# One hand-written order for all engines of a transformer block, written anew for each kind of iteration

## The reference

```
x = attention(ln(x), ln(x), Wq1, Wkv1, Wo1) + x      # 16 heads of 16 columns, 1024 keys
x = attention(ln(x), ctx, Wq2, Wkv2, Wo2) + x        # 16 heads, 154 keys
h, g = split(ln(x) @ Wff1 + bff1)                    # 256 -> 2 x 1024
x = (h * g * sigmoid(1.702 * g)) @ Wff2 + bff2 + x
x = softmax((x @ Wq.T + bq) @ (ctx @ Wk.T + bk).T) @ (ctx @ Wv.T + bv) + x
```

## Time and profile before

| | |
|---|---|
| median of 3 runs | 1716.65 us (1714.28 to 1716.99) |
| span of the profiled execution, first to last instruction | 1710.7 us |
| iterations 9 to 15 (everything in them) | 96.7 to 96.9 us each |
| iterations 17 to 19 | 93.7 us each |
| iterations 5, 6, 7 | 75.9, 65.9, 72.3 us |
| tail | 160.7 us |
| ScalarE's copy of a values tile (lines 1101 and 1161), mean | 0.37 us |

### The profile page before, as it was taken

How to read it: one execution, slowest core, us unless ns; L and a number is a source line. 1 busy time by engine, 2 the same in 40 slices (tenths; PEclk the granted TensorE clock), 3 DMA queues, 4 the chain that set the end, 5 groups by cost and what they waited for, 6 DMA issues and landing times.

```text
span 1710.7 us, 33819 instructions
## 1 busy us (share of the span) xinstructions
PE 1609.0 (94%) x12897; PEld 1019.8 (60%) x12897; DVE 1120.2 (65%) x2221; ACT 996.5 (58%) x2024; POOL 269.4 (16%) x344
## 2 busy tenths in 40 slices
PE   6799999999999999999999999999999999998887
PEld 5444445575756666575756666565656556564666
DVE  4466786867667685867667685867677676824333
ACT  3345767656666666656666666556666566663332
POOL 5201312112102021111102021101010010101100
PEclk9989999999999999999999999999999999997789
DMA  6913241446231231346221231336030321303200
GB/s 175 231 46 121 72 79 58 105 85 136 58 79 46 65 77 51 91 96 136 58 70 41 72 77 42 91 74 135 27 84 23 62 60 38 78 20 76 54 26 13
DMA packets 171647, 129.37 MB, mean 76 GB/s; under 512 B 40751, under 2 KB 161885, under 8 KB 171229
## 3 DMA queue, kind: packets, MB, share of 16 engines
q1 hardware_dynamic: 171421, 127.19, 31.1%
q10 hardware_dynamic: 64, 0.02, 0.0%
HBM read 78.92 MB, written 47.71 MB: 74 GB/s over the span
## 4 chain that ended last, share of the span: by engine, by line
PE 71%; DVE 18%; ACT 5%; issue 3%; DMA 2%; SPq 1%; POOL 0%; DVEq 0%; ACTq 0%; POOLq 0%
PE ps_o L1736 11%; PE ps_max L1702 10%; PE ps_last L1647 9%; PE ps_s L1724 9%; DVE mxh L1373 8%; PE ps_last L1656 6%; PE ps_cross L1615 4%; PE ps_pre L1511 3%; PE ps_pre L1519 3%; DVE mx L1298 3%; PE ps_cross L1601 2%; PE ps_last L1685 2%; DVE th L1330 1%; ACT probs L1152 1%; PE ps_last L1519 1%
## 5 line engine op out<-in xcount | busy, mean ns | idle before, releaser
L1373 DVE TENSOR_REDUCE mxh<-ps_max 128x1 f32<-128x512 f32 x1024 | 659.0, 683 | 221.6 <-PE ps_max L1702 217.7
L1152 ACT ACTIVATE probs<-ps_s 128x512 f32<-128x512 f32 x1024 | 581.1, 597 | 311.7 <-PE ps_s L1724 210.7
L1702 PE MATMUL ps_max<-kst,qst 96*128 96x512 bf16 x1024 | 363.4, 385 | 21.5 <-DVE mxh L1373 15.2
L1724 PE MATMUL ps_s<-qst,kst 98*128 98x256 bf16 x2048 | 371.6, 274 | 6.5 <-ACT probs L1152 4.9
L1736 PE MATMUL ps_o<-probs,vg 128*17 128x256 f32 x4096 | 270.0, 382 | 0.1
L1724 PEld LDWEIGHTS ps_s<-qst,kst 98*128 98x128 bf16 x2048 | 171.7, 98 | 155.7 <-ACT probs L1152 57.9
L1702 PEld LDWEIGHTS ps_max<-kst,qst 96*128 96x128 bf16 x1024 | 94.8, 97 | 143.7 <-DVE mxh L1373 94.0
L1330 DVE SCALAR_TENSOR_TENSOR th<-th,gb 128x256 f32<-128x256 f32 x128 | 66.2, 517 | 151.9 <-ACT gb L1124 151.9
L1736 PEld LDWEIGHTS ps_o<-probs,vg 128*17 128x17 f32 x4096 | 94.1, 96 | 112.2 <-issue 48.3
L1093 ACT ACTIVATE probs<-ps_cross 77x512 f32<-77x512 f32 x224 | 132.4, 591 | 31.7 <-PE ps_cross L1601 30.9
L1647 PE MATMUL ps_last<-y_hi,wff_hi 128*128 128x256 f32 x448 | 140.4, 313 | 10.4 <-DVE hT L1333 7.9
(11 more groups left out here) (265 smaller groups left out, 2016.4 us busy)
## 6 DMA issues: line engine op xcount, KB each, us to landing
parts_s<-qk_parts SPq DMA_DIRECT2D x28, 384.0 KB, 3.8
o_s<-o_sb SPq DMA_DIRECT2D x64, 128.0 KB, 2.8
o_s<-o_sb SPq DMA_DIRECT2D x32, 256.0 KB, 2.2
oT<-o_s SPq DMA_DIRECT2D x62, 128.0 KB
den<-o_s SPq DMA_DIRECT2D x62, 128.0 KB
kst<-parts_s SPq DMA_DIRECT2D x16, 384.0 KB, 5.2
kst<-parts_s SPq DMA_DIRECT2D x48, 128.0 KB, 5.7
qst<-parts_s SPq DMA_DIRECT2D x64, 96.0 KB, 2.7
```

The lines of the kernel that those rows point to most:

```text
L1152: nc.scalar.activation(probs[:, step % PR, 2 * pair:2 * pair + 2, :].rearrange("p j q -> p (j q)"), ps_s[pair][:, :], ACT.Exp, scale=SCALE ...
L1373: nc.vector.tensor_reduce(mxh[:, i // 2, i % 2:i % 2 + 1], ps_max[i % 2][:, :], AX_X, ALU.max).then_inc(g_mx, 1)
L1702: mm(ps_max[i % 2][:, :], qst[0:ROWS, h, q * P:(q + 1) * P], kst[0:ROWS, h, k * 512:(k + 1) * 512], start=True, stop=True).then_inc(g_mt, 1)
L1724: last = mm(ps_s[pair][:, j * CH:(j + 1) * CH], kst[:, h, kt * P:(kt + 1) * P], qst[:, h, :], start=True, stop=True)
```

## The change

`EARLY` and `END_ORDER` go. Iterations 4, 5, 6 and 7 get strings of their own (`FIRST`, `SECOND`, `THIRD`, `FOURTH`), with only the letters that they have; iteration 20 gets `FINAL`, the tail gets `ENDING`, and `STEADY` and `LATE` are written anew. Setup steps are now letters `s` in the strings. One `walk` serves the tail too, where c and g are `cross` of 14 and 15, and l, k, j are `last` of 13, 14 and 15. The counts of the shared letters run on through the whole kernel (`seen`), so the same work is done in the same order within each kind; the lead of M over S is two units as before. No instruction is added, dropped or changed: what changes is where each stands in its engine's queue.

```diff
-LEAD = 2
-
-
-EARLY = (
-    "SSMMSMSMMSMSMSMcSVMo"
-    "SMSMSccSccMScMVMSumcSMMmQScmc"
-    "SVTpcSScuMpMScOVSMScVpSSMcoMcV"
-    "ScMpMSMSMpMcMSSMupMcSMVcMSSMcppQcTVOlc"
-    "SlmMcSMclSMllScMMScSMMcSSmMcV"
-    "SMmScMSMVMScMSMSmlMlulllcSMQVTcS"
-    "SMlllllcMSmMMcVcSMOSMcmSMSdMlSVlSM"
-    "SlMVMSoSMMoSSMSMMQSSOlVlxTlielflVlll"
+
+
+
+FIRST = (
+    "ppssssssssspspspspspMsMMMMsMMpMMMMsMMMMMQsTMMMsMMMMMsMMMMMMMMQT"
 )
 
+SECOND = (
+    "ppSMMMSMMMSMSMSMSsSSMMVMSMSVMSMSsMSSVSQTSSMMSsSMOpVSMMouVMSMpSMS"
+    "MpMSsSMMpMSMVSMMSQpSSsSSTVSMSMSuVOMSsMSMSVMSMpSMMSMMSsMSMSMMMVQS"
+    "STVSMMSsMSSMMSuVOMSSMMSsSMVMSMSVSMSMooSMSMSsMSQSTVOV"
+)
+
+THIRD = (
+    "ppSMMMuSMMMSoMSMmSMSsSSMMVMSMSVMSMSsMSSmVSQTSSMMSsSMOpmVSMMouVMS"
+    "MpSMSMpMSsSMMpMSMVSMMSQpSSsmSSTVmSMSMSuVOMSsMSMSmVMSMpSMmMSMMSsM"
+    "SMSMmMMVQSSTVSMMmSsMSSMMSuVOMSSMMSSMVMSMSVSMSxMooSMSMSMSQSTVOV"
+)
+
+FOURTH = (
+    "ppSMMMuSMMMSocMcSMmSMScSSMcMcVMcSMcSVMScMScMSSmVSQcTcSSMMSSMOpcc"
+    "mVSMMocuVMScMpSMScMpMcSSMMpcMSMVcSMMSQpSScmSSTVmScMSMSuVOcMSMScM"
+    "SmVcMSMpScMmMcSMMScMcSMSMcmcMMVcQSSTVcSMMmScMSSMcMSuVcOMSSMcMSSM"
+    "VMSMSVSMSxdMooSMSMeSMSQSTifVOV"
+)
+
 STEADY = (
-    "lMMMSMcSMSMSMScScSMSMc"
-    "SlcMVoclSMcMSucSlMMlSVSSmMMSQc"
-    "SVTSlcSMcMlcmVScMMSSmOpplSoSMpcccV"
-    "SMSlSVpMMlSMuMcpScSMMlcpMMlVMMScQSlcpTc"
-    "SSpmcuMSSMclcSMVcSSmMulScOMM"
-    "SclMMVVMMcSmlMSMlMSMclMMlQScSmVTcSSMcmMcl"
-    "SSMVMScSMOlSMmMlcMoSlMSMVSMM"
-    "SVSdMSMSMxSMQSlSSVioTVOefl"
+    "MpMSSuMlSMSMMclSMoSMSMuSMSMSMccVlcMmMcSlcMSMScVSSQlccSSTlVScScMS"
+    "MlSSOVMcMcpSlSScVcMpMSSlVpcMSMSlcpMcMlocMSMVSlMcSSMpcMSMQlTcpcMm"
+    "SMSlcVOSMScMSlMmSocVVcmSSMMlMpMmlcSSMuMulmcMSMSlcMlSSmMcSMQSoVTc"
+    "VMOcmmMSMclMSMScMlMSMScMSMlSVSMdMSlSMSMVMSSxMQilSTVefOlV"
 )
 
 LATE = (
-    "MMlSSoMSMSMSMSMMSSMcccMl"
-    "SMcluVScMSMclMcMSlVSSMVcQmScST"
-    "SlccSMSoMlSScVMcMSOlScmVMMSlMcVM"
-    "SSlcScMmSSppMSMpcMplpcpSMMppcSl"
-    "SuMcMVQlcSTcSScmMMlcVMMSOuSclSuSc"
-    "SMMSVlmMcMlMMmScSlSMMSVMcMmSoMlMQcSlVTcM"
-    "SScmcMSSMVMmMSlcMSSMlOclSMVMMd"
-    "SxSMlMSSMVMSMlSMSieQVSlfTOoV"
+    "lMMSSMSMuSMSMMlSMSMcScScSMMlVcMMclMcMSSMcQVlSSTVScScSolMcSSMclVS"
+    "McOcmMSlSScMcSMlmSVMScMlSMcMSVcSSMMlcMoMScSluMmSVMcQSlSTcVScSScm"
+    "OMmMlSMcVSSMmclMScSmMcoSSMlSMMVMclMmuMMSclMMlMclSSuQVTcSlMcmSMVc"
+    "OMMSSclMMcxSMSMlVMSMSSMSMlSMdSMVSMMSQeloSTilVfVO"
 )
 
+FINAL = (
+    "lMMSSMSMuSMSMMlSMSMcScScSMMlVcMMclMcMSSMcQVlSSTVScScSolMcSSMclVS"
+    "McOcmMSlSScMcSMlmSVMScMlSMcMSVcSSMMlcMoMScSlMmSVMcQSlSTcVScSScmO"
+    "mlScVSSmclScSmcoSSlSVclmScllclSSVcSlcmSVcOSSclcxSSlVSSSSlSdSVSSe"
+    "loSilVfVO"
+)
+
+ENDING = (
+    "oclcclccgccmccccccclcmlcccccllccmcccmcmlccmclmlmccllmccxllccllcl"
+    "llkldilgglggglkggglgegglggkflkggkgggggggkgggkjggggjgkglggkgkgkkd"
+    "kikkkkjjkjjkkjkjjjjjjjjekjjjjjkjkjfkjjjkj"
+)
+
 
 def order_of(n):
 
-    return EARLY if n < LAST_LAG else STEADY if n < NCH else LATE
+    if n < LAST_LAG:
+        return (FIRST, SECOND, THIRD, FOURTH)[n - MAX_LAG]
+    return STEADY if n < NCH else LATE if n < END - 1 else FINAL if n < END else ENDING
 
...
-SETUP_AT = ([i for i in range(M_STEP)] + [SLOTS // 2 + 2 * i for i in range(6)]
-            + [SLOTS + 2 + 3 * i for i in range(NCT + 1)]
-            + [2 * SLOTS - 2] + [2 * SLOTS + 2 + 3 * i for i in range(KD * FF1_PIECES)])
-
-
-def setup_steps(n, slot):
-
-    return SETUP_AT.count(SLOTS * (n - MAX_LAG) + slot)
+VSTEPS = 2
 
 
 END = NCH + ATT_LAG
-END_MID = NCH - 1
-END_CROSS = dict(c=NCH - 2, d=NCH - 1)
-END_LAST = dict(x=NCH - 3, y=NCH - 2, z=NCH - 1)
-END_LOADS = dict(q="d", i="y", j="y", k="y", l="y", r="z", s="z", t="z", u="z")
-END_ORDER = "cmcccccccxcxccxccccxcmcxmcxcccxcccccmcmmxxymccxmmxccxzdcxcyqxccxcxxxxxidddddxdjddxddddkdxxldxddyddddyxyddddddddyddydddzdydryyyysytyyzyyzzyyuzyzyzzzzzzzzyzzzzzyzyzyyzzzz"
+SHARED = "SVMTQOouxdief"
...
-def max_tile(n, k):
-
-    unit = HG * (n - ATT_LAG) + k // (2 * PAIRS) + LEAD
-    return (unit if 0 <= unit < NU else None), k % (2 * PAIRS)
-
-
-def max_unit(n, k):
-
-    return max_tile(n, 2 * PAIRS * k)[0]
+def chains_of(n):
+
+    if n == END:
+        return dict(m=("mid", NCH - 1), c=("cross", NCH - 2), g=("cross", NCH - 1), l=("last", NCH - 3),
+                    k=("last", NCH - 2), j=("last", NCH - 1))
+    at = dict(p=("pre", n), m=("mid", n - MID_LAG), c=("cross", n - CROSS_LAG), l=("last", n - LAST_LAG))
+    return {letter: (kind, o) for letter, (kind, o) in at.items() if 0 <= o < NCH}
...
-        def run(body, iterations):
-
-            for n in iterations:
-                body(n, n % 2, stages(n), stages(n - 1)[2], stages(n + 1))
-
-        def walk(n, flags, setup, pre, mid, cross, last, work):
-
-
-            has_pre, has_max, has_att, has_mid, has_cross, has_last = flags
-            chains = dict(
-                p=pre(n) if has_pre else None, m=mid(n - MID_LAG, has_pre) if has_mid else None,
-                c=cross(n - CROSS_LAG) if has_cross else None, l=last(n - LAST_LAG) if has_last else None)
-            seen = dict.fromkeys(order_of(n), 0)
+        def run(body):
+
+            for n in range(MAX_LAG, END + 1):
+                body(n, stages(n))
+
+        def walk(n, setup, kinds, work, seen):
+
+            chains = {letter: kinds[kind](o) for letter, (kind, o) in chains_of(n).items()}
             for letter in order_of(n):
-                k = seen[letter]
-                seen[letter] += 1
-                if letter in work:
-                    work[letter](k)
-                elif letter in chains and chains[letter] is not None:
-                    next(chains[letter])
-                if letter == "S" and k % 2:
-                    for _ in range(setup_steps(n, k // 2)):
-                        next(setup)
-            assert all(next(chain, None) is None for chain in chains.values() if chain is not None)
-
-        def walk_end(mid, cross, last, loads=lambda letter: None):
-
-
-            chains = {letter: cross(o) for letter, o in END_CROSS.items()}
-            chains.update({letter: last(o) for letter, o in END_LAST.items()})
-            chains["m"] = mid(END_MID, False)
-            for letter in END_ORDER:
-                if letter in END_LOADS:
-                    loads(letter)
+                if letter == "s":
+                    next(setup)
+                elif letter in SHARED:
+                    k = seen[letter]
+                    seen[letter] += 1
+                    if letter in work:
+                        work[letter](k)
                 else:
                     next(chains[letter])
-            assert all(next(work, None) is None for work in chains.values())
+            assert all(next(chain, None) is None for chain in chains.values())
...
-                def store_unit(k):
-                    if 0 <= first + k - 1 < NU and (flags[2] or att_before):
-                        store_o(first + k - 1)
-
-                def load_unit(k):
-                    done = first + k - 1
-                    if 0 <= done and done + HG < NU:
-                        load_stack(done + HG)
-                        if (done // HG + 1) % CPB == 0:
-                            load_values((done // HG + 1) // CPB, done % HG)
-
...
+            def load_unit(done):
+                load_stack(done + HG)
+                if (done // HG + 1) % CPB == 0:
+                    load_values((done // HG + 1) // CPB, done % HG)
...
+            def exp_tile(k):
+                step, pair = divmod(k, 2)
```

More of the change, by code:

```diff
@@ L819, in _ @@
             head()
             setup_work = setup()
-            run(body, range(MAX_LAG, END))
-            store_o(NU - 1)
-            walk_end(mid, cross, last, end_loads)
+            seen = dict.fromkeys(SHARED, 0)
+            run(body)
             sp.wait_ge(c_outst, NCH * 16)
@@ L1404, in _ @@
-            run(body, range(MAX_LAG, END))
-            walk_end(mid_by(1 - (END_MID + MID_LAG) % 2, True), cross_by(True), last, end_inverses)
+            seen = dict.fromkeys(SHARED, 0)
+            run(body)
         @block.tensor
@@ new lines, in max_scores @@
+            def max_scores(k):
+                unit, i = divmod(k, 2 * PAIRS)
+                c, g = divmod(unit, HG)
+                h, q, half = g * G + i // 2 // TT, i // 2 % TT, i % 2
+                if i == 0:
+                    pe.wait_ge(g_stack[g], (c + 1 + c // CPB + 1) * 64)
+                    pe.wait_ge(g_slo, unit)
+                pe.wait_ge(g_mx, unit * 2 * PAIRS + max(0, i - 1))
+                mm(ps_max[i % 2][:, :], qst[0:ROWS, h, q * P:(q + 1) * P],
+                   kst[0:ROWS, h, half * 512:(half + 1) * 512], start=True, stop=True).then_inc(g_mt, 1)
@@ new lines, in max_turn, with scores @@
+            def max_turn(unit):
+                pe.wait_ge(g_mp, unit + 1)
+                nc.tensor.transpose(ps_max[0][0:PAIRS, 0:P], mxq[:, :], ident[:, :]).then_inc(g_mT, 1)
+            def scores(k):
+                step, pair = divmod(k, 2)
+                unit, kt = divmod(step, KT)
```

(33 more changed lines are left out.)

206 lines of the change are left out of this document (56 added, 150 removed).

## The result

The changed kernel takes 1691.75 us (median of 4 runs, 1690.69 to 1693.78) against 1715.47 of the kernel before beside it (4 runs); the ratio is 0.9882, 95% interval 0.9857 to 0.9907. Forecast was -10 us, measured some -20 to -24. The profiled execution has a span of 1692.0 us and took 1693.78, so 1.8 us lie around it, as in every run of the kernels here; the 5.95 us that I put around the span of before were for the most part the difference between one execution and the median. The span after is 18.7 us under that of before.

The account below looks back on a forecast made before the run. No engine is full: TensorE sets the time and loses some waiting where work of one partner is bunched. Terms -8.4 + 4.0 - 1.9 - 1.2 - 3.5 + 1.0 = -10.0 us gave 1706.6 us, 8-in-10 range 1683 to 1729.

Parts of the forecast that it names:

- Part 1: Iterations 5 to 20: 38 fewer separate stretches of values matmuls on TensorE, 0.22 us each, -8.4 us.
- rival (a): Mainly iterations 8 to 20: TensorE's waits themselves shrink by a quarter, 30 us more gain, 1677 us; chance 0.22.
- Part 2: Iterations 5 to 7: more maxima and a layer norm bunched ahead of the first V, charged at +4.0 us.
- Part 3: Way into the tail, end of iteration 20: x issued ahead of d ends a late-stack wait, -1.9 us.
- Part 4: Inside the tail: a moved transposition, -1.2 us, and feed-forward pieces moved into the last cross, -3.5 us.
- Part 5: Iteration 4: two p first make VectorE stand at pre_x ahead of the setup's subtraction, +1.0 us.
- SP's stand at u: STEADY: SP held at the second u some 9 us of TensorE's work, delaying loads of m; costed at nothing.
- (b): Joins' gain given back to waits for VectorE or ScalarE; only parts 3 and 4 count, 1716 us; chance 0.14.
- Rival (c): STEADY's iteration ends: late denominators cost about 3 us in each of eight iterations, 1731 us; chance 0.22.

Follow-up runs that it names:

- ff_closer: All new strings, but in iterations 8 to 15 the sixth feed-forward piece stands ahead of a projection and five small items; iteration 10 takes 96.4 us instead of 94.2.
- d_ahead_of_x: All new strings, but in iteration 20 d stands directly ahead of x, as before the change; iteration 20 takes 87.3 us instead of 86.0.
- new_4_to_7: New strings for iterations 4 to 7 alone, old ones for all others; ratio 0.9993 to the kernel before.
- i_ahead_of_x: All new strings, but in iterations 10 and 14 i stands directly ahead of x; 1695.89 us, 0.9923 of the kernel before.
- improved2: New strings with cross ending sooner in iterations 10 and 14, d and x early in 18, i or u moved in 9, 13, 16 to 19; 1685.62 us, 0.9849.
- ff_moved: All old strings, but in iterations 8 to 15 two feed-forward pieces stand some four and seven letters later; 1743.14 us, 1.0183 of the kernel before.
- after_again: The new kernel run once more, nothing changed; 1696.15 us, 0.9899 of the kernel before.
- improved: New strings with i ahead of x in 10 and 14, d and x early in 18, i or u moved in 9, 13, 16 to 19; 1693.43 us, 0.9900.
- improved3: improved2 with a milder shift in iterations 10 and 14, the last three steps of cross two to five letters sooner than the new kernel's; 1683.97 us, 0.9829.

## Why the prediction came out as it did

The sign was right and the mechanism that I named first, fewer switches, is real. What was wrong is the size, half of what was measured or less. By the ratios of the four kernels that take over one kind of iteration each, I was 5 us too high in 4 to 7 (+4.1 forecast, -1.2 measured), 5 us too high in 8 to 15 (-5.3, -10.3), 5 us too low in 16 to 19 (-1.8, +3.4) and 3 us too high in 20 and the tail (-7.0, -10.1).

- **Part 1** (-8.4 for 38 joins): right per join, 0.25 us measured. But "I take all of it: waits sit elsewhere" made joins the whole gain of iterations 8 to 15. A clean iteration gained 2.5 us, 0.7 by joins; the rest, 1.8 us, are waits that shrank, first of all those at the feed-forward pieces, whose 1.9 us stand in the earlier trace rows. This is the step that failed: I weighed the waits only "ahead of the first V", where both strings are alike, and gave the others to rival (a). ff_closer shows that one such place costs 2.2 us an iteration; that the hidden tiles are the larger part of the 1.8 us is read from the totals of the groups, and no run takes the waits apart one by one.
- **Part 2** (+4.0): +2.9 us with 0.9 of joins in it, so +3.8. Right in this trace, though it sits mostly in iteration 5 (+2.1). It is a good execution: the fourteen traces with these strings take 215.7 to 220.9 us for 5 to 7, the six with the old ones 213.7 to 214.2. In eight of the fourteen the clock falls for 3 to 10 us in iterations 6 and 7, in none of the six, and where it falls in 6 that iteration takes 68.5 us instead of 66.0. No bunch was weighed for that.
- **Part 3** (-1.9): 1.1 us by d_ahead_of_x; the earlier trace rows had its wait put down to no engine, and the new tail opens with none. Iteration 20 is 3.7 us shorter in all, and as much in the other traces; the rest was not taken apart.
- **Part 4** (-1.2 and -3.5): the second is right. From the start of the last values of `cross` to the end 68.6 us became 65.0, as two pieces of 1.84 us left. The first isn't there: from the tail's start to the first scores of the last `cross` old tails take 66.4 to 70.1 us, new ones 67.3 to 70.0. The wait of the earlier trace rows went to the projection before it (1545.49, first row below). Tail lengths mix this with the clock: the last three rows are the tail of the old string in new_4_to_7, and of the new one in i_ahead_of_x and improved2. Over all traces old tails take 154.5 to 160.6 us, new ones 146.3 to 156.5.

```profile
1545.49 3.78 PE L1454 MATMUL ps_last<-wo,oT 128*128 128x256 f32 x8 [1.62 <-DVE oT L1211]
...
1626.98 1.06 PE L1550 MATMUL ps_cross<-probs,v 77*17 77x256 f32 x16
```

```profile
1549.00:1706.40 157.40, 131.69 (x782) 99.19 (x782) 60.62 (x132) 52.83 (x119) 16.92 (x25) 0.84 0.13 37
```

```profile
1542.90:1692.30 149.40, 124.09 (x786) 95.25 (x782) 59.91 (x132) 52.81 (x120) 17.37 (x25) 0.89 0.13 39
```

```profile
1530.70:1677.00 146.30, 119.67 (x786) 92.37 (x782) 60.32 (x132) 52.55 (x120) 16.81 (x25) 0.93 0.15 39
```

- **Part 5** (+1.0): wrong sign. Iteration 4 gained; 1 us between the context's transposition and the first maxima (19.8 to 18.7), some 2 behind it, and 1.6 in the head, which varies by as much between profiles of the same strings there. The slip that I named is there, TensorE waits 1.75 us for it at 51.64, but the order before waits longer further on (0.29, 1.16 and 1.16 us, for pre_x and the copies of the projections). It takes 19.8 us in all six traces, the new one 18.6 to 19.3 in twelve of fourteen. The 2 us behind it are mostly the clock: before, TensorE waits 1.37 us at T, where a setup step stands now, and the clock is at 0.50 from 82.0 to 85.4. ff_moved has the old strings there, the same wait and a clock of 1.00, and takes 25.65 us for this stretch instead of 27.15; the new kernel takes 25.38. Neither gain outlives iterations 5 to 7: iteration 8 starts at 306.3 to 309.1 us with the old strings and at 307.3 to 312.7 with the new ones, and the new kernel's own trace is the best of the latter.
- **SP's stand at u, at nothing**: no wait of TensorE's for loads of m shows. Right.
- **Rival (a)** came out in part, for the waits; **(b)** is out. **Rival (c)** is real in mechanism and in price per place (0.6 to 5.5 us), but not "by 1.2 us of room in STEADY": in undisturbed iterations the chain fits. It breaks most where x brings nine loads, but behind four as well (9 and 17 here, 13 with 97.7 us in after_again). "LATE and FINAL keep 10 us here" was false comfort, as iteration 19 shows: distance in TensorE's work says nothing of what is in the DMA queue ahead. So two things that I left out nearly cancel in 8 to 19: clean iterations gain 2.5 us in eight places and 1.3 in four, 25 us together where I had 7, and the late denominators took back 19, of which the kernel before had lost 2 already. That these lines sum to -8.4 us against my -7.1 is luck.

Not settled: what the late denominators in iterations 9, 13 and 17 hang on (with u and i moved, 9 and 17 take 94.2 and 93.6 us in `improved`, but 95.4 and 94.3 in improved2 and 95.0 and 93.9 in improved3, and 17 takes 92.9 in after_again with nothing moved), and why iterations 5 and 20 came out as they did beyond the terms.
